# Value products of two attention quads given back to back at every second quad, with four probability slots

## The chip, the cores and the metric

The kernel runs on one core of a Trainium2 chip. The metric is the device time of one execution in microseconds (us). The kernel before has a median of 1106.15 us over 3 runs (1104.24 to 1106.32).

## The reference

Two transformer layers, each with the norm behind the residual sum, on x of shape (2, 1024, 256), 16 heads of width 16, float32. Cut to what matters:

```python
# layer 0: causal attention, then a feed-forward with ternary weights
dots = einsum('bhid,bhjd->bhij', q, k) * scale ; causal mask
out  = einsum('bhij,bhjd->bhid', softmax(dots), v)
x = layernorm(x + out @ w_out + b_out) ; x = layernorm(x + ffn0(x))
# layer 1: 16 query heads, 4 key heads, slope times distance added to the scores,
# a band of +-32 around the diagonal and the first 64 rows and columns left out
qk = q k^T * scale + slope * (-|i - j|) ; qk = where(band or global, -1e9, qk)
out = softmax(qk) @ v
x = layernorm(x + out @ Wo + bo) ; x = layernorm(x + ffn1(x))
```

## The kernel before, in words

Each layer is a block in which five engines run in parallel, ordered by semaphores. The attention of a layer is cut into N = 8 groups: 2 batches times 4 groups of 4 heads (HG = 4). A group is cut into quads: one quad is one tile of 128 keys against one half (512) of the queries, for the 4 heads of the group. Layer 0 has 12 quads (half 0 has 4, half 1 has 8, since the mask is causal; near the diagonal a quad has 384, 256 or 128 columns instead of 512). Layer 1 has 16 quads, 8 of 448 columns and 8 of 512; the last of each half has 64 key rows. A step of a quad is:

- "exp": TensorE writes one head's shifted scores (`shifted`, lines 1039 to 1059) into a PSUM bank, and ScalarE writes their exponential into the probabilities `prob` (lines 1005 to 1007). There are two banks for this, 4 and 5 (`T_BANKS`, line 688), and four in the last group. TensorE waits before a shifted product until the exponential that used its bank is done (lines 1120 to 1122).
- "max": TensorE writes the scores of one head and 128 queries (`score`, line 1029) for the group that comes next, and VectorE takes the row maximum (lines 940 to 942), with two slots of two banks each. There are 32 such units per group, 2 or 3 per quad.
- "values": TensorE multiplies the quad's probabilities with the values (`values`, lines 1061 to 1079). Each head is a product with 32 output rows, so four heads stand side by side in the array and write bank 6 in four strips. They are float32 and read as 8 records. Line 1135 waits for GpSimd's mask (lines 871 and 877) where the quad touches the diagonal or the band.
- "evict": ScalarE copies bank 6 to SBUF at the end of each half (line 1014). "norm": TensorE transposes the copy (line 1147) and VectorE divides (lines 971 and 973).

The function `plan` (line 125 on) writes out by hand one order of these steps for a group, and every engine goes through that same list and does its own part. The values of quad n - 1 stand behind the exponentials of quad n. The values of a group's last quad, its last eviction and its last norm are done at the first and second quad of the group that follows.

`prob` holds two quads, quad q in slot q % 2. ScalarE waits before a quad's first exponential for the values of the quad two before (line 1003). SyncE loads the operands of a later group when the values of the one before are all done (line 814), and GpSimd stages values then (line 883). The last group also has the preparation of the output projection in its list (`with_preparation`).

Of the kernel before, what the change touches and what calls it, by code (L numbers as in the profile page):

```python
# [20 lines left out]
F32 = mybir.dt.float32  # L21
# [4 lines left out]
P = 128  # L26
# [6 lines left out]
HG = 4  # L33
NG = H // HG
N = B * NG
E = 1024
KE = E // P
CH = 512
# [86 lines left out]
def plan(layer, group):  # L125

    quads = quads_of(layer)
    nq, nu = len(quads), len(units_of(layer))
    rows_at = nq - KEY_TILES_AHEAD[layer.index]
    lead = nu * KEY_TILES_AHEAD[layer.index] // nq  # L130
    stream = [(k, 1) for k in range(lead if group >= 1 else 0, nu)] if group + 1 < N else []
    stream_next = [(k, 2) for k in range(lead)] if group + 2 < N else []
    late, last = group >= 1, group == N - 1
    steps, given, given_next = [], 0, 0
    tail = [("values", nq - 1), ("evict", 1), ("norm", 1)]
    for n, (half, kt) in enumerate(quads):
        due = min(len(stream), -(-len(stream) * (n + 1) // rows_at))
        due_next = -(-len(stream_next) * (n + 1 - rows_at) // (nq - rows_at)) if n >= rows_at else 0
        if n == rows_at and stream:
            steps.append(("parts", 0, 1))  # L140
        for h in range(HG):
            steps.append(("exp", HG * n + h, 0))
            upto = given + -(-(due - given) // (HG - h))
            steps += [("max", u, later) for u, later in stream[given:upto]]
            given = upto
            upto = given_next + -(-(due_next - given_next) // (HG - h))
            steps += [("max", u, later) for u, later in stream_next[given_next:upto]]
            given_next = upto
        if n == 0 and late:
            steps += [(what, k, -1) for what, k in tail[:2]]  # L150
        if n == 1 and late:
            steps.append((*tail[2], -1))
        if n == 1 and not last:
            steps.append(("stage", 0, 1))
        if group <= 2 and layer.index == 1 and n in CUT_QUADS:

            steps.append(("cut", 2 * group + CUT_QUADS.index(n), 0))
        if n >= 1:
            steps.append(("values", n - 1, 0))
            if quads[n - 1][0] != half:  # L160
                steps.append(("evict", quads[n - 1][0], 0))
        if n >= 2 and quads[n - 2][0] != quads[n - 1][0]:
            steps.append(("norm", quads[n - 2][0], 0))
        if n == rows_at and stream:
            steps.append(("rows", 0, 1))
        first = RESIDUAL_GROUP[layer.index]
        if first <= group < first + 4 and n in RESIDUAL_QUADS[layer.index]:
            steps.append(("residual", 4 * (group - first) + RESIDUAL_QUADS[layer.index].index(n), 0))
    if last:
        steps += [(what, k, 0) for what, k in tail]  # L170
        steps = with_preparation(steps, nq)
    return steps
# [498 lines left out]
def attend(nc, sem, K, L, dram, prep, before):  # L671


    i = L.index
    tag = str(i)
# [4 lines left out]
    NU, NX, NQ = len(units), HG * len(quads), len(quads)  # L680
# [11 lines left out]
    MH = HG if i == 0 else HG // 2  # L692
# [17 lines left out]
    values_done = sem("values_done" + tag)  # L710
# [4 lines left out]
    with ExitStack() as st:  # L715
        table, maxes, vst, prob, mpart, mrow, ot, rec = (K.table, K.maxes, K.vst, K.prob, K.mpart, K.mrow, K.ot, K.rec)
# [5 lines left out]
            before.proj = proj  # L722
        opening = opening_of(L, proj)

        def exp_slots(n):
            return LAST_T_BANKS if n == N - 1 else T_BANKS

# [93 lines left out]
        def _(pool):  # L821
# [38 lines left out]
            def step(group, steps):  # L860
                for what, k, later in steps:
                    n = group + later
                    if what == "exp" and k % MH == MH - 1 and diagonal[k // HG] is not None:

                        pool.wait_ge(exp_done, n * NX + (k + 1))
                        half, kt = quads[k // HG]
                        a, b = diagonal[k // HG]
                        j0, rows = key_tile(L, kt)
                        cells = prob[0:rows, k // HG % 2, k % HG + 1 - MH:k % HG + 1, a - half * CH:b - half * CH]
                        if i == 0:  # L870
                            nc.gpsimd.affine_select(out=cells, in_=cells, pattern=[[0, HG], [1, P]],  # L871
                                                    compare_op=ALU.is_ge, fill=zero, base=0, channel_multiplier=-1
                                                    ).then_inc(masked, 1)
                        else:
                            off = a - (j0 - WIN)
                            bits = cells.bitcast(I32)
                            nc.gpsimd.tensor_tensor(bits, bits, keep[0:rows, off:off + b - a].unsqueeze(1)  # L877
                                                    .to_broadcast((rows, MH, b - a)), ALU.mult
                                                    ).then_inc(masked, 1)
                    elif what == "stage":  # L880
                        if group >= 1:

                            pool.wait_ge(values_done, group * NQ)
                        if n == NG:

                            pool.wait_ge(proj.v_done, (2 - i) * len(proj.v_units))
                        stage(n, n % BUFS)
                    elif what == "cut":

                        j, cols = k // 2, slice(k % 2 * E, (k % 2 + 1) * E)  # L890
                        pool.wait_ge(w_loaded, 16 * (j + 1))
                        nc.gpsimd.tensor_copy(K.wffn[:, j, 0, cols], wf[:, cols]).then_inc(w_cut, 1)
                        pool.wait_ge(w_cut, 2 * k + 1)
                        nc.gpsimd.tensor_tensor(K.wffn[:, j, 1, cols], wf[:, cols],
                                                K.wffn[:, j, 0, cols].bitcast(F32), ALU.subtract).then_inc(w_cut, 1)
                    elif what == "residual":
                        if k == 0:

                            pool.wait_ge(proj.xt_full, len(proj.turns))
                            pool.wait_ge(K.tri_loaded, 16 * 5)  # L900
                        nc.gpsimd.tensor_tensor(K.x[:, k, :], K.x[:, k, :], K.bias[:, i, :], ALU.add
                                                ).then_inc(residual, 1)
                    elif what == "inverse":
                        prep.inverse(pool, k, 0)
                    elif what in Projection.STEPS:
                        proj.pool(pool, what, k)
                    elif what in FeedForward.STEPS:
                        before.pool_tail(pool, what, k)
# [83 lines left out]
        def _(act):  # L992
            def step(group, steps):
                for what, k, later in steps:
                    n = group + later
                    if what == "exp":
# [1 line left out]
                        lo, hi = columns_of(L, half, kt)  # L998
                        rows = key_tile(L, kt)[1]
                        q = k // HG  # L1000
                        if k % HG == 0 and n * NQ + q >= 2:

                            act.wait_ge(values_done, n * NQ + (q - 1))
                        act.wait_ge(t_full, n * NX + (k + 1))
                        nc.scalar.activation(prob[0:rows, q % 2, k % HG, lo % CH:lo % CH + hi - lo],  # L1005
                                             ps[0:rows, t_bank(n, k), lo % CH:lo % CH + hi - lo],
                                             ACT.Exp).then_inc(exp_done, 1)
                    elif what == "evict":
# [19 lines left out]
        def _(pe):  # L1028
# [29 lines left out]
                        start = False  # L1058
                return last

            def values(qd, par):

                half, kt = quads[qd]
                lo, hi = columns_of(L, half, kt)
# [9 lines left out]
                for h in range(HG):  # L1074
                    last = nc.tensor.matmul(ps[32 * h:32 * h + 32, O_BANK, lo % CH:lo % CH + hi - lo],  # L1075
                                            vst[:, par, vt_, h % v_heads, :],
                                            prob[:, qd % 2, h, lo % CH:lo % CH + hi - lo],
                                            start=opening and not uniform, stop=True, skip_group_check=True)
                return last

            def step(group, steps):
                for what, k, later in steps:
# [41 lines left out]
                    elif what == "values":  # L1124
# [8 lines left out]
                        pe.wait_ge(exp_done, n * NX + HG * (k + 1))  # L1133
                        if diagonal[k] is not None:
                            pe.wait_ge(masked, HG // MH * (n * upto[-1] + upto[k]))
                        values(k, b).then_inc(values_done, 1)
                    elif what == "norm":
                        pe.wait_ge(evicted, n * 2 + (k + 1))

# [445 lines left out]
def memory(shared, at, L):  # L1585
# [20 lines left out]
    K.kop = at((101632, 122112)[i], "kop" + tag, [P, BUFS, L.key_sets, T], BF16)  # L1606
    K.vst = at((126208, 164992)[i], "vst" + tag, [P, BUFS, TB + i, v_heads, 2 * HD], F32)
    K.prob = at(171392, "prob" + tag, [P, 2, HG, CH], F32)
    K.maxes = at((23040, 164864)[i], "maxes" + tag, [P, HG, TB], F32)
    K.mpart = at((22528, 168448)[i], "mpart" + tag, [P, 2, P // 2], BF16)  # L1610
    K.mrow = at((22784, 168704)[i], "mrow" + tag, [P, P], BF16)
# [110 lines left out]
```

## Time and profile before

| | before |
|---|---|
| median of 3 runs | 1106.15 us (1104.24 to 1106.32) |
| the profiled execution's own time | 1099.92 us |
| its span | 1098.2 us |
| mean granted TensorE clock | 0.973 |
| TensorE busy | 994.7 us (91%) |
| VectorE busy | 697.1 us (63%) |
| ScalarE busy | 605.9 us (55%) |
| GpSimd busy | 346.5 us (32%) |
| attention groups, layer 0 | from 84 to 355 us of the span |
| attention groups, layer 1 | from 535 to 941 us of the span |

PE is TensorE, PEld its weight loads, ACT is ScalarE, DVE VectorE, POOL GpSimd. Matmuls are pipelined and the ends of their records are modelled, so a busy TensorE is not TensorE at its peak, and the start of a record tells more than its end. A row of the timeline merges neighbouring instructions of one kind on one engine: its start is that of the first, its duration reaches to the end of the last, and x gives their number. The brackets at a row's end hold the idle time of the engine before it and what ended it.

### The profile page before, as it was taken

The page shows a single profiled execution, that of the slowest core. Times are in us where ns is not written, and L with a number is a line of the kernel's source. Part 1 is how long each engine was busy: PE and PEld are TensorE (multiplying, and loading weights), DVE is VectorE, ACT ScalarE, POOL GpSimd, SP SyncE. Part 2 cuts the span into 40 slices and gives each one's busy share as a digit, 9 for nine tenths or more (in the row PEclk, how much of TensorE's full clock was granted, in tenths as well). Part 3 has the DMA queues.
Part 4 walks back from the last instruction along what each step waited for, and adds up shares of the span by engine and source line. Part 5 has one row for each costly group of instructions (what it writes and reads, how often), then busy time and mean ns, then how long its engine had stood idle before and what let it go on. Part 6 is the DMA issues. An engine that isn't in the chain of part 4 may idle for free. (4 is left out here: it accounts for less than half of the span.)

```text
span 1098.2 us, 17969 instructions
## 1 busy us (share of the span) xinstructions
PE 994.7 (91%) x6546; PEld 517.9 (47%) x6546; DVE 697.1 (63%) x1535; ACT 605.9 (55%) x1204; POOL 346.5 (32%) x414
## 2 busy tenths in 40 slices
PE   6688999999988999877799999999999999899995
PEld 4342333333324788653333343433334344698885
DVE  2877877777735566457787777777777724235322
ACT  4335666676665434333566777777776767323321
POOL 3031312222211434321344353524334252324331
PEclk9898999999999899997899999999999999999999
DMA  7552110112000200024433050303211000000001
GB/s 252 168 172 70 59 43 18 59 58 59 2 1 1 74 15 1 23 90 110 148 94 133 30 162 2 124 4 121 71 54 36 1 2 1 1 1 20 20 1 39
DMA packets 32979, 64.19 MB, mean 58 GB/s; under 512 B 6079, under 2 KB 22351, under 8 KB 30516
## 3 DMA queue, kind: packets, MB, share of 16 engines
q1 hardware_dynamic: 31548, 58.47, 17.3%
q0 software_dynamic: 1072, 3.80, 1.0%
q8 instruction: 52, 0.85, 0.3%
q10 hardware_dynamic: 272, 0.79, 0.2%
q14 instruction: 35, 0.29, 0.1%
HBM read 50.45 MB, written 12.32 MB: 57 GB/s over the span
## 5 line engine op out<-in xcount | busy, mean ns | idle before, releaser
L1005 ACT ACTIVATE prob<-ps 128x512 f32<-128x512 f32 (+6 forms) x896 | 442.7, 537 | 211.4 <-PE ps L1048 203.7
L1048 PE MATMUL ps<-qop,kop 98*128 98x512 bf16 (+15 forms) x1376 | 302.4, 291 | 21.3 <-ACT prob L1005 7.6
L1034 PE MATMUL ps<-kop,qop 96*128 96x512 bf16 (+3 forms) x896 | 255.7, 359 | 33.2 <-DVE maxes L940 26.6
L1048 PEld LDWEIGHTS ps<-qop,kop 107*128 107x128 bf16 (+2 forms) x1376 | 114.4, 98 | 278.2 <-ACT prob L1005 200.7
L1075 PE MATMUL ps<-prob,vst 128*32 128x512 f32 (+4 forms) x1792 | 211.2, 543 | 3.9 <-POOL prob L877 2.6
L940 DVE CUSTOM_DVE_ANT_0 sums<-ps,tri 128x128 bf16<-128x128 f32 (+7 forms) x256 | 183.7, 754 | 43.6 <-PE ps L1034 42.3
L940 DVE CUSTOM_DVE_ANT_0 sums<-ps,table 128x960 bf16<-128x960 f32 x128 | 148.0, 1156 | 80.4 <-PE ps L1034 65.8
L877 POOL TENSOR_TENSOR prob<-prob,keep 128x384 int32<-128x384 int32 (+2 forms) x144 | 122.6, 853 | 220.7 <-ACT prob L1005 218.2
L1466 PE MATMUL ps<-xs,wffn 128*128 128x512 f32 x640 | 157.0, 401 | 3.7 <-PEq L715 2.2
L940 DVE CUSTOM_DVE_ANT_0 tri<-ps,table 128x960 bf16<-128x960 f32 x128 | 147.5, 1152 | 3.6 <-PE ps L1034 3.5
L1466 PEld LDWEIGHTS ps<-xs,wffn 128*128 128x128 f32 x640 | 120.4, 191 | 31.5 <-issue 5.1
L1367 POOL TENSOR_TENSOR hs<-hf,hs 128x512 fp32r<-128x512 f32 x64 | 82.8, 1295 | 158.8 <-ACT hs L1393 158.2
L1034 PEld LDWEIGHTS ps<-kop,qop 96*128 96x128 bf16 x896 | 79.0, 99 | 104.1 <-DVE maxes L940 58.6
L871 POOL TENSOR_SCALAR_AFFINE_SELECT prob<-prob 128x512 f32<-128x512 f32 x64 | 40.9, 639 | 205.8 <-ACT prob L1005 205.8
L1487 PE MATMUL ps<-wffn,hs 128*128 128x256 f32 x640 | 80.6, 287 | 7.1 <-POOL hs L1367 7.1
L1487 PEld LDWEIGHTS ps<-wffn,hs 128*128 128x128 f32 x640 | 78.9, 195 | 9.1 <-POOL hs L1367 8.4
L1393 ACT CAST hs<-hf 128x512 fp32r<-128x512 f32 x64 | 39.3, 614 | 72.4 <-PE ps L1487 66.3
L1075 PEld LDWEIGHTS ps<-prob,vst 128*32 128x32 f32 x1792 | 35.7, 108 | 50.9 <-issue 35.1
L1431 DVE SCALAR_TENSOR_TENSOR hf<-ps,sg 128x512 f32<-128x512 f32 x32 | 22.0, 690 | 46.6 <-PE ps L1466 46.6
L1400 ACT ACTIVATE sg<-ps 128x512 f32<-128x512 f32 x32 | 19.2, 599 | 54.0 <-PE ps L1466 54.0
L940 DVE DVE_READ_ACCUMULATOR2_ANT maxes<- 128x1 f32 x512 | 42.4, 83 | 0.0
L615 PE MATMUL ps<-prob,w 128*128 128x512 f32 x80 | 38.0, 607 | 1.3 <-DVE staging L542 1.3
(103 smaller groups left out, 686.4 us busy)
## 6 DMA issues: line engine op xcount, KB each, us to landing
table<-in_table SPq DMA_DIRECT2D x32, 464.0 KB, 5.1
qop<-q_parts SPq DMA_DIRECT2D x96, 128.0 KB, 2.6
kop<-k_parts SPq DMA_DIRECT2D x48, 128.0 KB, 2.6
kop<-k_parts SPq DMA_DIRECT2D x48, 96.0 KB
q_parts<-qop SPq DMA_DIRECT2D x8, 384.0 KB, 2.9
q_parts<-kop SPq DMA_DIRECT2D x8, 384.0 KB, 2.6
x<-in_x SPq DMA_DIRECT2D x4, 512.0 KB, 5.5
out<-x SPq DMA_DIRECT2D x4, 512.0 KB, 2.9
```

Source lines behind the costliest of these rows:

```text
L615: last = nc.tensor.matmul(ps[:, self.bank(what, k), :], w[:, half, m * P:(m + 1) * P], src[:, half, t0:t0 + CH], start=(half == 0), stop=( ...
L871: nc.gpsimd.affine_select(out=cells, in_=cells, pattern=[[0, HG], [1, P]], compare_op=ALU.is_ge, fill=zero, base=0, channel_multiplier=-1) ...
L877: nc.gpsimd.tensor_tensor(bits, bits, keep[0:rows, off:off + b - a].unsqueeze(1) .to_broadcast((rows, MH, b - a)), ALU.mult).then_inc(mask ...
L940: nc.vector.tensor_tensor_reduce(out=sums[k % 2][:, lo:hi], in0=scores, in1=mask, scale=1.0, scalar=LOWEST, op0=ALU.add, op1=ALU.max, accu ...
L1005: nc.scalar.activation(prob[0:rows, q % 2, k % HG, lo % CH:lo % CH + hi - lo], ps[0:rows, t_bank(n, k), lo % CH:lo % CH + hi - lo], ACT.Ex ...
L1034: last = nc.tensor.matmul(ps[:, S_BANK + 2 * (k % S_SLOTS) + a // CH, a % CH:a % CH + b - a], qop[0:RD, par, h, i0:i0 + P], kop[0:RD, par, ...
L1048: return nc.tensor.matmul(ps[0:rows, bank, a % CH:a % CH + b - a], lhs, rhs, start=start, stop=True, skip_group_check=True)
L1075: last = nc.tensor.matmul(ps[32 * h:32 * h + 32, O_BANK, lo % CH:lo % CH + hi - lo], vst[:, par, vt_, h % v_heads, :], prob[:, qd % 2, h, ...
L1367: nc.gpsimd.tensor_tensor(self.hidden(e, 1), hf[:, u % 2, :], self.hidden(e, 0).bitcast(F32), ALU.subtract).then_inc(self.h_lo, 1)
L1393: nc.scalar.copy(self.hidden(e, 0), hf[:, u % 2, :]).then_inc(self.h_hi, 1)
L1466: last = nc.tensor.matmul(ps[:, 2 * (u % 2) + which, :], weights[a][:, k, e * P:(e + 1) * P], prep.xs[:, c % 2, b, k, :], start=(n == 0), ...
L1487: last = nc.tensor.matmul(self.K.ps[:, 4 + half, (j % 2) * D:(j % 2 + 1) * D], self.hidden(e, b)[:, j * P:(j + 1) * P], self.wdown[a][:, e ...
```

## The change

The values of two quads are given together. In groups 0 to 6, at quads n = 2, 4, 6, ..., the values of quads n - 2 and n - 1 are given one behind the other, and at odd quads none are given. The values of the last two quads of a group are given at the first quad of the next group, with the eviction behind them. The last group keeps its single quads, one behind the exponentials.

The probabilities get a second array of the same size, `prob_far`, so that quad q of groups 0 to 6 has slot q % 4; the last group uses the two slots of `prob` as before. ScalarE's wait before a quad's exponentials is for the values of the quad four before (two before in the last group, from its third quad on). The order of exponentials, maxima, evictions and norms within the list is the same.

```diff
@@ plan
     tail = [("values", nq - 1), ("evict", 1), ("norm", 1)]
+    pair = [("values", nq - 2), *tail]
...
         if n == 0 and late:
-            steps += [(what, k, -1) for what, k in tail[:2]]
+            steps += [(what, k, -1) for what, k in pair[:3]]
         if n == 1 and late:
-            steps.append((*tail[2], -1))
+            steps.append((*pair[3], -1))
...
+        if last and n >= 1:
+            steps.append(("values", n - 1, 0))
+        elif not last and n >= 2 and n % 2 == 0:
+            steps += [("values", n - 2, 0), ("values", n - 1, 0)]
         if n >= 1:
-            steps.append(("values", n - 1, 0))
             if quads[n - 1][0] != half:
                 steps.append(("evict", quads[n - 1][0], 0))
@@ attend
+        def tile(n, q):
+
+            slot = q % 2 if n == N - 1 else q % 4
+            return (prob if slot < 2 else K.prob_far)[:, slot % 2, :, :]
@@ gpsimd, the mask
-                        cells = prob[0:rows, k // HG % 2, k % HG + 1 - MH:k % HG + 1, a - half * CH:b - half * CH]
+                        cells = tile(n, k // HG)[0:rows, k % HG + 1 - MH:k % HG + 1, a - half * CH:b - half * CH]
@@ scalar, the exponential
-                        if k % HG == 0 and n * NQ + q >= 2:
-
-                            act.wait_ge(values_done, n * NQ + (q - 1))
+                        back = 2 if n == N - 1 and q >= 2 else 4
+                        if k % HG == 0 and n * NQ + q >= back:
+
+                            act.wait_ge(values_done, n * NQ + (q + 1 - back))
...
-                        nc.scalar.activation(prob[0:rows, q % 2, k % HG, lo % CH:lo % CH + hi - lo],
+                        nc.scalar.activation(tile(n, q)[0:rows, k % HG, lo % CH:lo % CH + hi - lo],
@@ tensor, values
-                                            prob[:, qd % 2, h, lo % CH:lo % CH + hi - lo],
+                                            tile(n, qd)[:, h, lo % CH:lo % CH + hi - lo],
@@ memory
     K.prob = at(171392, "prob" + tag, [P, 2, HG, CH], F32)
+    K.prob_far = at((49152, 77056)[i], "prob_far" + tag, [P, 2, HG, CH], F32)
```

## Rows read from the trace of the kernel before

**Rows 1.** Page, busy us (share of the span) xinstructions of each engine.

```profile
PE 994.7 (91%) x6546; PEld 517.9 (47%) x6546; DVE 697.1 (63%) x1535; ACT 605.9 (55%) x1204; POOL 346.5 (32%) x414
```

**Rows 2.** Busy time in two stretches: one group of layer 0, one of layer 1.

```profile
259.43:292.44 33.01, 30.49 (x203) 10.42 (x201) 24.81 (x72) 22.35 (x50) 5.63 (x9) 1.00 0.14 41
700.31:749.38 49.07, 48.35 (x391) 18.28 (x390) 38.19 (x72) 35.28 (x67) 18.41 (x25) 1.00 0.22 70
```

**Rows 3.** Waits: who waited for whom, us in total, times, longest.

```profile
ACT prob L1005 <- PE ps L1048: 203.7, 260, 8.0
PEld ps L1048 <- ACT prob L1005: 200.7, 443, 1.0
```

**Rows 4.** Timeline of one quad, layer 1, first half: start us, us, engine line op.

```profile
709.58 0.96 PE L1075 MATMUL ps<-prob,vst 128*32 128x448 f32 x8
...
710.47 0.10 PEld L1048 LDWEIGHTS ps<-qop,kop 107*128 107x128 bf16 x1 [0.73 <-ACT prob L1005]
...
710.67 0.57 PE L1034 MATMUL ps<-kop,qop 96*128 96x448 bf16 x2
...
710.93 2.12 ACT L1005 ACTIVATE prob<-ps 128x448 f32<-128x448 f32 x4 [0.67 <-PE ps L1048]
711.08 0.35 PE L1048 MATMUL ps<-qop,kop 107*128 107x448 bf16 x1
...
711.38 1.16 DVE L940 CUSTOM_DVE_ANT_0 sums<-ps,table 128x960 bf16<-128x960 f32 x1 [0.63 <-issue]
...
712.07 0.10 PEld L1048 LDWEIGHTS ps<-qop,kop 107*128 107x128 bf16 x1 [0.44 <-ACT prob L1005]
...
712.36 0.96 PE L1075 MATMUL ps<-prob,vst 128*32 128x448 f32 x8
...
712.46 1.15 DVE L940 CUSTOM_DVE_ANT_0 tri<-ps,table 128x960 bf16<-128x960 f32 x1
```

**Rows 5.** Timeline of one quad, layer 1, second half.

```profile
727.57 1.06 PE L1075 MATMUL ps<-prob,vst 128*32 128x512 f32 x8
...
728.56 0.40 PE L1048 MATMUL ps<-qop,kop 107*128 107x32 bf16 x2
...
729.06 2.30 ACT L1005 ACTIVATE prob<-ps 128x512 f32<-128x512 f32 x4 [0.76 <-PE ps L1048]
729.21 0.39 PE L1048 MATMUL ps<-qop,kop 107*128 107x32 bf16 x2
...
730.29 0.11 PEld L1048 LDWEIGHTS ps<-qop,kop 107*128 107x128 bf16 x2 [0.34 <-ACT prob L1005]
...
730.62 1.07 PE L1075 MATMUL ps<-prob,vst 128*32 128x512 f32 x8
```

**Rows 6.** Timeline of an eviction and of the turn of its output.

```profile
721.08 0.96 PE L1075 MATMUL ps<-prob,vst 128*32 128x448 f32 x8
...
722.11 0.59 ACT L1014 COPY ot<-ps 128x512 f32<-128x512 f32 x1 [0.29 <-PE ps L1075]
...
722.59 2.17 ACT L1005 ACTIVATE prob<-ps 128x512 f32<-128x512 f32 x4
...
724.06 1.07 PE L1075 MATMUL ps<-prob,vst 128*32 128x512 f32 x8
...
725.55 0.38 PE L1048 MATMUL ps<-qop,kop 107*128 107x512 bf16 x1
```

**Rows 7.** Timeline of layer 0: value products of 128 columns.

```profile
289.75 0.42 PE L1075 MATMUL ps<-prob,vst 128*32 128x128 f32 x8
...
290.10 0.34 PE L1048 MATMUL ps<-qop,kop 98*128 98x384 bf16 x1
```

**Rows 8.** Timeline of the quad with 64 key rows, layer 1.

```profile
716.03 0.38 PE L1048 MATMUL ps<-qop,kop 107*64 107x448 bf16 x1
...
716.85 0.38 PE L1048 MATMUL ps<-qop,kop 107*64 107x448 bf16 x1
```

More of the change, by code:

```diff
@@ L1059, in shifted, with values @@
                 return last
-            def values(qd, par):
+            def values(n, qd, par):
                 half, kt = quads[qd]
@@ L1135, in step @@
                             pe.wait_ge(masked, HG // MH * (n * upto[-1] + upto[k]))
-                        values(k, b).then_inc(values_done, 1)
+                        values(n, k, b).then_inc(values_done, 1)
                     elif what == "norm":
```

## The prediction

> **What bounds the kernel now.** I read the busy shares first, then the two attention stages by window, then the waits, then the timeline of single quads. The page shows TensorE busy 91% of the span and ScalarE 55% [rows 1], which invites the reading "TensorE is the bound". One group of 12 quads in layer 0 takes 33.01 us and one of 16 quads in layer 1 takes 49.07 us, at full granted clock, with TensorE busy 30.49 and 48.35 us [rows 2]. But a busy record includes the time in which a matmul drains, and the waits tell another story: ScalarE waited 203.7 us for the shifted scores of line 1048, and TensorE's weight loads for that line waited 200.7 us for ScalarE's exponentials [rows 3]. Two engines that wait for each other by the same amount are in a loop.
>
> The timeline shows the loop [rows 4]. Call s0 to s3 the four shifted products of a quad, e0 to e3 their exponentials, V a quad's value products, m a maximum's score product. V starts at 709.58. s0 follows at 710.47, 0.89 later. e0 starts at 710.93, 0.46 after s0, and ScalarE had been idle for 0.67. Four exponentials take 2.12, 0.53 each. There are two score banks, so s3 can't be given before e1 is done: that is at 710.93 + 1.06 = 711.99, and the weights of s3 load at 712.07, 0.08 later, after an idle 0.44 put down to ScalarE. The next V follows at 712.36, 0.29 later. So the period is 0.89 + 0.46 + 1.06 + 0.08 + 0.29 = 2.78 us, and each term is a step that waits for the one before. e2 and e3 are not in it: they run beside V. In the second half of layer 1, with 512 columns, the same sum is 0.99 + 0.50 + 2 x 0.575 + 0.08 + 0.33 = 3.05 us [rows 5]. TensorE has slack in it: beside V it is the two-bank hand-over with ScalarE that sets the pace.
>
> **The change, part by part.** It removes, adds and moves no arithmetic. At each second quad it gives two sets of value products one behind the other, and none at the quad between. The groups concerned are 0 to 6 of each layer: 7 x 6 = 42 pairs in layer 0 and 7 x 8 = 56 in layer 1, 98 in all.
>
> Gained by pairing: one exit from the value products and one entry. After V of 128 columns the next product starts 0.35 later [rows 7]; after 512 columns, 0.99 [rows 5]. That is 0.64 for 384 columns, 0.00167 us each, which is four passes at 2.4 GHz. So 128 columns stream for 0.21 and the exit costs 0.14. At the entry V starts 0.29 behind s3, where the score product m starts 0.20 behind s0 [rows 4]: 0.09. Together 0.23 per pair. The cost of V behind V appears in no row. It is at least the streaming, 0.75 for 448 columns, and at most the streaming with exit and entry, 0.98. I take 0.75, since between two V nothing changes in the shape of the tiles, and keep the other end for the range.
>
> Lost by pairing: the cover of e2 and e3. Chain of a pair in the first half of layer 1, from the first V at 0. The second V at 0.75, s0 at 0.75 + 0.89 = 1.64, e0 at 2.10 to 2.63. Meanwhile ScalarE still has only two exponentials to do, since the banks are two as before: e2 and e3 of the last quad end at 0.70, so it idles for 1.40, and twice the old 0.67 is 1.34. The longer pause gives nothing back. s1 follows s0 by 0.61, as 711.08 after 710.47 [rows 4], since m lies between; s1 2.25, e1 2.71 to 3.24; s2 at 2.86, e2 3.32 to 3.85; s3 waits for e1: 3.32, e3 3.85 to 4.38. No V here: the next quad's s0 needs the bank of e2, 3.85 + 0.08 = 3.93, e0 4.39 to 4.92; s1 4.54 (0.61 behind), e1 5.00 to 5.53; s3 at 5.61, V at 5.90. Two old periods are 5.57. So **+0.33 us per pair**: two more exponentials on the path (1.06) and 0.24 of TensorE pacing, against one 0.46 + 0.08 + 0.29 and the exit of 0.14 saved.
>
> For the second half, with 0.64 from s0 to s1 (729.21 after 728.56 [rows 5]): streaming 0.85 + 0.99 = 1.84, e0 2.34, e1 2.98 to 3.56, e2 3.62 to 4.20, next s0 4.28, e0 4.78, s1 4.92, e1 5.42 to 5.99, s3 6.07, V 6.40, against 6.10: **+0.30**.
>
> The quads with 64 key rows stand at the end of each half of layer 1, before the boundary. Their s0 to s1 is 0.82 instead of 0.61 [rows 8]. Singly that delays the loop once (0.21), in a pair twice: +0.21 more, two per group.
>
> The eviction and the turn (norm) come twice per group. Before, ScalarE's copy starts 0.07 after V ends and holds the next exponential for 0.48 [rows 6]; it lies in the pause. In a pair the second V ends at 0.85 + 1.06 = 1.91, so the copy starts at 1.98 and e0 at 2.46 instead of 2.34: 0.12 lost, and e0 is what is queued behind it. The four transposes stretched V to s0 to 1.49 (724.06 to 725.55 [rows 6]), 0.50 more than 0.99. In the new order they follow a quad that has no V: s3 at 3.76, plus 0.20, plus 0.50 gives 4.46 instead of s0 at 4.28. Total 0.18 lost where about 0.46 was paid before (3.51 from V at 724.06 to V at 727.57 against 3.05 [rows 5, 6]): a gain of 0.27, two per group, 0.54.
>
> The other queues. VectorE: maxima follow each other by 1.08 (711.38 to 712.46 [rows 4]), 4.3 in a pair of 5.9, and the first starts 0.71 behind its m (710.67 to 711.38): m at 1.84 and 2.45 end at about 3.7 and 4.8, the third m (4.13) finds its slot free, the fourth (4.74) waits for 4.87, which moves s2 and not s3. Free; if VectorE were 0.4 later it would set V. GpSimd's masks of the second quad must be there at 5.90, and e3 of that quad ended at 4.38, against 0.70 and 2.78 before: a little less margin, still 1.5 us. SyncE's operand loads and GpSimd's staging wait for the last values of a group, now one V (0.9 us) later, a group (33 or 49 us) ahead of need. Four slots for the probabilities: ScalarE's wait is for values two pairs back, never last. All three at nothing; the cover is the group's length.
>
> Sum. Layer 1, per group: 4 x 0.33 + 4 x 0.30 + 0.42 - 0.54 = 2.40, times 7 = 16.8. Layer 0, per group, with full quads like those of the second half (its short quads have shorter exponentials but then wait for the wide maxima): 6 x 0.30 - 0.54 = 1.26, times 7 = 8.8. Total **+25.6 us**. The last groups, the projections and the feed-forward are the same code. On the profiled execution, 1099.92 us with a span of 1098.2, that gives 1125.5. That execution is 6.2 below the median of 1106.15 and under the lowest of the three runs (1104.24). From the median: 1131.8, said as 1132.
>
> The Trainium skill, TensorEngine Tiling (Array Packing), Key Properties, says that changing the tiling mode, not just the tile, drains the TensorEngine. The exit of 0.14 [rows 5, 7] agrees. By that rule alone the change is a gain; what it would give is the first rival.
>
> **Rivals.** (1) *TensorE is the bound after all, and the drain saved is time saved.* 98 x 0.23 = 22.5 us less: 1083.6. For it: 48.35 busy of 49.07 [rows 2]. Against it: the idle 0.67 before e0 and 0.44 before s3 in each quad [rows 4], and the period that adds up without any TensorE work but V and s3. It decides if ScalarE's exponentials ran ahead of TensorE, that is, if s0 to s3 of the quad without V didn't wait for their banks. Chance 0.10.
> (2) *A draw.* The pacing of TensorE in the pair, 0.24, is hidden. Then a pair costs 6 x 0.53 + 1.64 + 0.46 + 0.08 + 0.29 = 5.65, +0.08, and in the second half +0.10; 98 x 0.09 - 28 x 0.27 = 1.3 us: 1107.5. For it: the queue of TensorE may give s1 early, since its bank is free. Against: rows of each quad show 0.61 with m between. Chance 0.07.
> (3) *The second V pays exit and entry like the first*, 0.23 more: +22.5, so 1154. For it: each V set ends with a signal and begins with waits. Against: they are met by then. Chance 0.06.
> (4) That the pairs aren't formed can't be: each engine's order is written out.
> The forecast has the rest, 0.77.
>
> **How the numbers follow.** Within the forecast, layer 0 may be 0 to 2.5 a group and the V behind V may cost some 0.15 more, which is 1115 to 1148. The range goes down to the draw at its lower part, 1108, and leaves out (1), most of what lies within 0.2% (2.2 us, about what a measurement of this kernel can tell from no change) and the top of (3). Faster: (1), and the low side of (2), 0.11. Same: the rest of (2), 0.06. Slower: 0.83.
>
> **What the new profile would show.** V sets starting 0.75 or 0.85 apart in pairs, then 5.9 us to the next pair in layer 1's first half and 6.4 in its second; a layer 1 group of 51.5 us and a layer 0 group of 34.3. ScalarE idle about 1.4 before the first exponential behind a pair, and almost none at the next quad. Exit rows between V and V gone. The turn's transposes off the path. I am wrong if the pair's period is under 5.57: then e0 to e3 of the quad between were not the path. I am wrong in a term if V to V isn't 0.75, or if s0 of the second quad starts later than 2.29 after that of the first (3.93 less 1.64).

## Result and profile after

The changed kernel takes 1125.22 us (median of 4 runs, 1121.18 to 1126.49), against 1105.2 for the kernel before beside it (1101.87 to 1106.32): a ratio of 1.0183, 95% interval [1.0151, 1.0215], so 20 us more. The profiled execution took 1124.03 us with a span of 1122.3; its counterpart of before had 1099.92 and 1098.2, so the two traces lie 24.1 us apart. The forecast was 25.6 more. The sign and the mechanism held; the sizes of several terms did not, and a term that the forecast didn't have, the granted clock, made up for part of what it had put too high.

The work is the same, as the page after shows (engine busy us, share, instructions), to be held against [rows 1]:

```profile
PE 995.3 (89%) x6546; PEld 531.8 (47%) x6546; DVE 694.3 (62%) x1535; ACT 609.7 (54%) x1204; POOL 346.3 (31%) x414
```

TensorE and ScalarE are busy for nearly as long as before (0.6 and 3.8 us more), in a span 24.1 us longer: nearly all of the time is waiting. By stretches (us, then PE, PEld, DVE, ACT, POOL busy, granted clock, DMA share, GB/s), group 0 of layer 0, one steady group of layer 0 and one of layer 1; the last two answer to [rows 2]:

```profile
85.37:134.16 48.79, 41.73 (x229) 13.95 (x230) 34.26 (x98) 26.96 (x57) 6.27 (x10) 0.87 0.15 43
236.26:270.30 34.04, 30.20 (x203) 11.16 (x202) 24.90 (x72) 22.75 (x50) 8.39 (x13) 1.00 0.15 45
719.77:769.74 49.97, 47.51 (x393) 19.15 (x390) 37.93 (x72) 35.29 (x67) 18.38 (x25) 1.00 0.22 69
```

The same stretch of group 0 in the kernel before, from its first shifted product to the same norm:

```profile
84.58:127.38 42.80, 39.01 (x230) 13.09 (x230) 34.42 (x98) 26.31 (x57) 6.28 (x10) 0.93 0.16 49
```

A steady group costs 1.03 us more in layer 0 and 0.90 more in layer 1, at full clock in both. Group 0 of layer 0 costs 6.0 more, at a lower granted clock (0.87 against 0.93). Followed through the trace, the first feed-forward starts 14.4 us later than before (0.8 of it before the attention, 6.0 in group 0, 5.1 in the next five groups, 2.5 in the rest), the output of layer 1's attention 22.6 later, and the end 24.1. The 0.8 ahead of the attention and the last 1.5 lie in code that the change leaves alone.

One pair in the timeline after, answering to [rows 4] (start us, us, engine line op):

```profile
726.42 1.71 PE L1085 MATMUL ps<-prob_far,vst 128*32 128x448 f32 x16
...
728.06 0.36 PE L1058 MATMUL ps<-qop,kop 107*128 107x448 bf16 x1
...
728.52 2.11 ACT L1015 ACTIVATE prob<-ps 128x448 f32<-128x448 f32 x4 [1.30 <-PE ps L1058]
...
729.27 0.75 PE L1058 MATMUL ps<-qop,kop 107*128 107x448 bf16 x2
...
730.25 0.36 PE L1058 MATMUL ps<-qop,kop 107*128 107x448 bf16 x1 [0.23 <-ACT prob L1015]
...
730.71 1.08 ACT L1015 ACTIVATE prob_far<-ps 128x448 f32<-128x448 f32 x2
...
731.26 0.11 PEld L1044 LDWEIGHTS ps<-kop,qop 96*128 96x128 bf16 x2 [0.48 <-DVE maxes L949]
...
731.68 0.54 PE L1058 MATMUL ps<-qop,kop 107*128 107x448 bf16 x2
...
731.85 0.10 PEld L1058 LDWEIGHTS ps<-qop,kop 107*128 107x128 bf16 x1 [0.28 <-ACT prob_far L1015]
...
732.15 1.71 PE L1085 MATMUL ps<-prob,vst 128*32 128x448 f32 x16
```

The two value sets stand together (16 records, 1.71 us), and s0 comes 1.64 behind their start, as forecast. ScalarE was idle for 1.30 before e0 (forecast 1.40). The second quad's s0 waits for ScalarE (the idle 0.23) and comes at 3.83 behind V (forecast 3.93). The next V is at 5.73 (forecast 5.90), against 5.57 for two single periods. Two waits end at the same moment before it. The fourth maximum's product waits for VectorE until 731.26, which puts s2 at 731.68 and s3 right behind it, at 731.87, and e1 ends in time for the weights of s3 at 731.85. So in this pair VectorE sets the last part of the path as much as ScalarE does.

### The profile page after: what moved, and what is told of

It is laid out like the page before. It is cut to its first block and busy times, and to the rows that moved or that the text cites. A ratio compares the mean times of both kernels' runs of the same rounds, so it can differ in the third digit from the quotient of the medians.

```text
span 1122.3 us, 17965 instructions
## 1 busy us (share of the span) xinstructions
PE 995.3 (89%) x6546; PEld 531.8 (47%) x6546; DVE 694.3 (62%) x1535; ACT 609.7 (54%) x1204; POOL 346.3 (31%) x414
## 5 line engine op out<-in xcount | busy, mean ns | idle before, releaser
L1015 ACT ACTIVATE prob<-ps 128x512 f32<-128x512 f32 (+2 forms) x504 | 258.3, 562 | 94.7 <-PE ps L1058 88.9
L1015 ACT ACTIVATE prob_far<-ps 128x512 f32<-128x512 f32 (+5 forms) x392 | 186.4, 503 | 119.9 <-PE ps L1058 113.1
L1085 PE MATMUL ps<-prob,vst 128*32 128x512 f32 (+2 forms) x1008 | 118.5, 579 | 3.9 <-POOL prob L886 2.6
L886 POOL TENSOR_TENSOR prob_far<-prob_far,keep 128x384 int32<-128x384 int32 (+2 forms) x70 | 52.8, 755 | 174.3 <-ACT prob_far L1015 173.7
L886 POOL TENSOR_TENSOR prob<-prob,keep 128x384 int32<-128x384 int32 (+3 forms) x74 | 69.7, 944 | 55.8 <-ACT prob L1015 54.0
L1085 PE MATMUL ps<-prob_far,vst 128*32 128x512 f32 (+3 forms) x784 | 78.7, 520 | 0.0
L880 POOL TENSOR_SCALAR_AFFINE_SELECT prob<-prob 128x512 f32<-128x512 f32 x36 | 23.2, 644 | 166.6 <-ACT prob L1015 166.6
L1085 PEld LDWEIGHTS ps<-prob,vst 128*32 128x32 f32 x1008 | 25.8, 110 | 51.6 <-issue 40.1
```

What stands on the lines that cost most here:

```text
L1015: nc.scalar.activation(tile(n, q)[0:rows, k % HG, lo % CH:lo % CH + hi - lo], ps[0:rows, t_bank(n, k), lo % CH:lo % CH + hi - lo], ACT.Exp ...
```

## Experiments

All medians of before below come from runs beside the kernel in question.

**One layer at a time.** A function `paired(layer, group)` decides which groups give values in pairs; the others give them singly, with four slots.

```diff
+def paired(layer, group):
+    return 0 <= group < N - 1 and layer.index == 1      # second kernel: == 0
...
-        if last and n >= 1:
+        if not paired(layer, group) and n >= 1:
             steps.append(("values", n - 1, 0))
-        elif not last and n >= 2 and n % 2 == 0:
+        elif paired(layer, group) and n >= 2 and n % 2 == 0:
```

> Pairs in layer 1 alone, single quads in layer 0. The loop theory (a pair lengthens the chain shifted product, exponential, shifted product, because the last two exponentials of the quad between lose their cover): a group of layer 1 takes 49.96 us as with the full change, against 49.07 before, so 7 x 0.9 and the end of the last group, 6 to 8 us over before, and layer 0's groups take 33.01. Rival, the second probability array or four slots cost by themselves: layer 0's groups are longer too (they also use four slots here), and the total is nearer 14.

Measured: ratio 1.0069 [1.0049, 1.0089], 1112.03 us against 1105.24, 6.8 more. The windows, a group of layer 0 and one of layer 1:

```profile
259.53:292.62 33.09, 30.57 (x203) 10.42 (x202) 24.81 (x72) 22.46 (x50) 5.63 (x9) 1.00 0.15 45
708.62:758.58 49.96, 47.49 (x391) 19.12 (x389) 37.93 (x72) 35.27 (x67) 18.35 (x25) 1.00 0.21 67
```

Layer 1 has the change's group, layer 0 that of before.

> Pairs in layer 0 alone, single quads in layer 1. The loop theory: layer 0's groups take 34.03 instead of 33.01, 7 us in all, and layer 1's take 49.07. The clock theory (pairs make TensorE pause longer at the start of layer 0 and the granted clock falls to half there, where the first group took 6 us more): another 6 us on top, 12 to 14 in all over before, with a granted clock of half speed in a stretch of group 0 or 7. Without the clock's part: 7.

Measured: ratio 1.0115 [1.0095, 1.0136], 1117.12 us, 11.9 more, just under the span expected with the clock's part and well over the 7 without it.

```profile
268.32:302.37 34.05, 30.27 (x204) 11.16 (x201) 24.81 (x72) 22.99 (x50) 5.63 (x9) 1.00 0.13 40
714.04:763.10 49.06, 48.34 (x390) 18.27 (x389) 38.19 (x72) 35.28 (x67) 18.40 (x25) 1.00 0.22 70
```

The mirror image. 6.8 and 11.9 add up to 18.7 of the 20, which is the whole within the intervals, and layer 0 has the larger part. These two runs also separate the order from the clock. Counted from the first exponential of a group to that of the next, layer 1's groups together took 6.9 us more in the first run, with no fall of the granted clock in them beyond that at their start, which the kernel before has too. In the second run groups 1 to 6 of layer 0 took 1.02 to 1.04 more each, and group 0 took 3.9 more (41.95 against 38.01), with one fall of the clock at 94.5 us. The full change has that fall and another at 118.4, and its group 0 took 5.6 more (43.59): one such fall costs 1.6 us here.

**Slots alone.** `paired` returns False; the two arrays and the wait four quads back stay.

> Four slots and the looser wait of ScalarE, values of single quads as before. The loop theory: no change, within 2 us of before, since ScalarE never waited last for the values. Rival, the far array costs something by its place: 7 x 12 + 7 x 16 quads, half of them in the far array, would cost above 2 us.

Measured: ratio 0.9993 [0.9976, 1.0009], 1103.8 us against 1105.24. The far array and the looser wait cost and give nothing. All of the loss comes from the order of the value products and from what that order brings about.

**A longer third product, a longer first product.** The most direct test of "TensorE isn't the bound, the loop is" puts the same added work at two places of the kernel before.

```diff
+                        if k % HG == 2 and n < N - 1:      # second kernel: == 0
+                            shifted(k, b, t_bank(n, k))
                         shifted(k, b, t_bank(n, k)).then_inc(t_full, 1)
```

> The kernel before; in groups 0 to 6 of both layers TensorE gives the third shifted product of each quad twice, to the same bank (the output is the same). That adds 0.19 to 0.22 us of TensorE work to 196 quads, some 36 us. The loop theory: it lies in the time in which TensorE waits for e1, so it costs 0 to 0.05 a quad, 0 to 8 us. Rival, TensorE's work is the bound: 30 to 40 us.

> The same for the first shifted product of each quad, which lies on the loop between the values and the first exponential. The loop theory and its rival both expect the full 0.17 to 0.22 a quad, 30 to 42 us; only together with the run of the third product does it tell them apart.

Measured: the third product twice, ratio 1.0067 [1.0043, 1.0091], 8.0 us more (1111.41 against 1103.4). The first product twice, ratio 1.032 [1.0291, 1.0349], 36.3 more. In the windows, first with the third product doubled, a group of layer 0 and one of layer 1:

```profile
263.45:297.06 33.61, 31.69 (x214) 11.10 (x213) 24.81 (x72) 22.31 (x50) 5.63 (x9) 1.00 0.14 41
708.99:758.49 49.50, 49.50 (x421) 20.24 (x421) 38.41 (x72) 35.31 (x67) 18.40 (x25) 1.00 0.21 69
```

and with the first doubled:

```profile
268.50:303.00 34.50, 32.09 (x215) 11.50 (x214) 24.85 (x72) 22.35 (x50) 5.63 (x9) 1.00 0.14 40
724.58:776.86 52.28, 51.62 (x422) 20.43 (x421) 38.38 (x72) 35.61 (x67) 18.43 (x25) 1.00 0.21 66
```

In layer 1 the same work costs (49.50 - 49.06) / 16 = 0.03 us a quad at one place and (52.28 - 49.06) / 16 = 0.20 at the other. With the third product doubled, layer 1's window has TensorE busy for 49.50 of 49.50 us and still took almost all of the added work for nothing: busy time that the records fill isn't the bound. The rival of the prediction, that TensorE's own work decides, falls here.

The same on the changed kernel:

> The full change with the third shifted product of each quad given twice in groups 0 to 6 (same output). Single quads paid 8.0 us for it, 0.04 a quad. The loop theory: in a pair the third product of the first quad is on the path, since the next quad's first product waits for the bank of e2, and that of the second quad delays the fourth product (the one before the values) by what is beyond the end of e1: 0.2 and 0.1 to 0.2 a pair, 98 pairs, 25 to 40 us over the change (45 to 60 over before). Rival, TensorE keeps the slack in pairs that it has in single quads: 8 us over the change (28 over before).

Measured: ratio 1.0328 [1.0292, 1.0365] to before. The change alone is at 1.0183, so 16 us over it, where single quads paid 8. It lies between the two expectations. The trace says which half was right:

```profile
737.77 1.71 PE L1085 MATMUL ps<-prob_far,vst 128*32 128x448 f32 x16
...
739.42 0.36 PE L1058 MATMUL ps<-qop,kop 107*128 107x448 bf16 x1
...
741.80 0.36 PE L1058 MATMUL ps<-qop,kop 107*128 107x448 bf16 x1 [0.42 <-ACT prob L1015]
...
742.62 0.11 PEld L1044 LDWEIGHTS ps<-kop,qop 96*128 96x128 bf16 x2 [0.29 <-DVE maxes L949]
```

The second quad's s0 stands at 4.03 behind V instead of 3.83. That is the first quad's third product, on the path as expected, 0.20 a pair. The group of layer 1 took 51.52 us, 1.56 over the change's for 8 pairs: 0.20 each, and nothing for the second quad. There the fourth maximum's product comes 0.82 behind s0, at 742.62, still waiting for VectorE, where it came 1.01 behind in the change (731.26 after 730.25): the second quad starts 0.20 later and VectorE doesn't, so the added product finds the 0.19 that the wait for VectorE had taken up, and s3 again stands 1.62 behind s0. So the theory was right on the first quad of a pair and wrong on the second.

**Maxima behind the second product.** The prediction put 0.24 us of the pair on TensorE's pacing, because a maximum's score product stands between s0 and s1. In single quads this can be taken away.

```diff
-            upto = given + -(-(due - given) // (HG - h))
+            upto = (given, min(due, given + 2), due, due)[h]      # the same for stream_next
```

> The kernel before with one thing moved: the first maximum of a quad stands behind the second shifted product instead of between the first and the second, so s1 follows s0 by 0.20 us instead of 0.61. The loop theory: e1 then starts as soon as ScalarE is free and ends about 0.10 earlier, and s3 and the next values with it: 0.08 to 0.10 per quad of layer 1 (112 quads), 9 to 11 us, and between nothing and 8 us in layer 0, where the wide maxima come late: 9 to 19 us less in all. Rival, TensorE's own work is the bound: the order inside a quad changes nothing, within 2 us of before. Third case: the two maxima side by side make VectorE the late one, and it is slower.

Measured: ratio 1.0015 [0.9995, 1.0035], 1105.14 against 1105.24: no change, so the expected 9 to 19 us was missed. (Two of the twelve executions took 1112.7 and 1113.1 at a mean granted clock of 0.953, the other ten 1103.8 to 1106.8.) The trace shows two effects that cancel. A group of layer 1 takes 47.48 instead of 49.07, 0.10 a quad, as expected. A group of layer 0 takes 33.74 instead of 33.01 (the next expectation says 33.47, a misreading of these 33.74), which I put down to the wide maxima, up to three a quad, without a run that shows it. Group 0 of layer 0 takes 3.6 more (41.57 against 38.01 from first exponential to first exponential), with the granted clock at its lower level until 96.5 us instead of 90.4, and group 0 of layer 1 gained nothing. So the move was tried in layer 1 alone, and on top of the change. In the next kernels all maxima of a quad stand behind the second product, `(given, due, due, due)[h]`, where above a third one stood behind the third.

> The kernel before with single quads; in layer 1 alone both maxima of a quad stand behind the second shifted product. With late maxima in both layers a group of layer 1 took 47.47 us instead of 49.06 and one of layer 0 33.47 instead of 33.01. The loop theory: layer 1's gain alone is kept, 7 x 1.6 = 11 us less than before (median near 1094). Rival, the median of 1105.1 with both was no sum of a gain and a loss: no change, within 2 us.

> The full change with the same move of the maxima in layer 1. The loop theory with VectorE in it: the pair's path is then s0 (V+1.64), e2's end (V+3.78), the next s0 (V+3.83), and the fourth maximum's product can't start before VectorE has done the second (V+4.98), so s2 and s3 of the second quad come at 5.5 and 5.7 and the next V at 5.9 to 6.0 instead of 5.73: a group of layer 1 takes 50 to 52 us, no gain over the change (0 to 10 us more), where single quads gain 1.6 a group. Rival, TensorE's pacing is all that costs in the pair: it gains as single quads do, 5.63 a pair and 8 to 11 us less than the change.

Measured, single quads: ratio 0.9968 [0.995, 0.9985], 1099.75 against 1103.4, 3.6 less and not 11. The steady groups took 47.48, but group 0, which has 32 maxima over 13 quads, took 54.7 instead of 53.3 between two marks (the first product with `ones` of group 0 and that of group 1). From the first exponential of the one to that of the other it is more: 57.8 instead of 54.5. The granted clock stood at its lower level for the first 8.8 us of it, until 552.3, and in the kernel before for the first 4.9, until 547.8. So the loss in group 0 is one of the clock too.

Measured, pairs: ratio 1.0273 [1.0245, 1.0301], about 10 us over the change, at the top of what was expected. Here the move gains nothing, and the timeline has the reason:

```profile
735.53 1.71 PE L1086 MATMUL ps<-prob_far,vst 128*32 128x448 f32 x16
...
737.17 0.55 PE L1059 MATMUL ps<-qop,kop 107*128 107x448 bf16 x2
...
739.36 0.80 PE L1059 MATMUL ps<-qop,kop 107*128 107x448 bf16 x2 [0.34 <-ACT prob L1016]
...
740.56 0.11 PEld L1045 LDWEIGHTS ps<-kop,qop 96*128 96x128 bf16 x2 [0.46 <-DVE maxes L950]
...
741.45 1.71 PE L1086 MATMUL ps<-prob,vst 128*32 128x448 f32 x16
```

The next s0 stands at V+3.83 and the next V at V+5.92, both as written down before. The fourth maximum waits for VectorE (the idle 0.46) and carries the last two shifted products with it. VectorE is busy for 62% of the change's span, yet four maxima squeezed into the part of a pair without values find two slots full. The steady group is 50.04 us, no more than 0.1 over the change's. Nearly all of the 10 us is in group 0 of layer 1 (58.6 instead of 53.6 between the marks, 63.9 instead of 55.1 from first exponential to first exponential). There the granted clock stayed at its lower level until 572.9, the first 15.7 us of the group, where the change has it for 4.9, and fell once more at 593.3.

> Late maxima in layer 1 from group 1 on, single quads. With late maxima in all of layer 1 the steady groups gained 1.58 each, but group 0, which has 32 maxima over 13 quads, took 54.68 instead of 53.30, and the median gained 3.6 only. The loop theory with VectorE in it: group 0 returns to 53.3, the others keep 1.58, so 1 to 2 us under the run with late maxima everywhere and 5 to 9 under before. Rival, group 0's 1.4 was chance: same as that run, 3 to 4 under before.

Measured: ratio 0.9926 [0.99, 0.9952], 1096.03 us against 1106.03. By the ratio that is 8 us less than before, within the 5 to 9 expected, and 4 to 5 under the run with late maxima everywhere, where 1 to 2 was expected: the marks had shown only part of what group 0 lost. Group 0 of layer 1 is back at 53.2 us between the marks, and at 54.5 from first exponential to first exponential, with 5.3 us at the lower clock at its start. The steady groups keep their gain:

```profile
701.76:749.25 47.49, 47.32 (x391) 18.34 (x390) 38.05 (x72) 33.95 (x67) 18.42 (x25) 1.00 0.22 72
```

This version, single quads with the maxima behind the second product in layer 1 from group 1 on, beats both kernels.

**The clock in group 0.**

> The full change, but group 0 of each layer keeps single quads. The full change is 20 us over before. Of its groups 1 to 6, layer 0 gives 6 x 1.03 and layer 1 6 x 0.9, 11.6 us. The clock theory: in layer 0's group 0 the profiled execution showed a granted clock of 0.84 against 0.93 from 84 to 127 us and took 6 us more instead of 1; without pairs there that goes, so 11 to 14 us over before, and group 0 has before's clock. Rival, the falls of the clock are chance and not the pairs': still 18 to 20 over before.

Measured: ratio 1.0125 [1.0098, 1.0152], 12.8 us over before and 6 to 7 under the change, within the 11 to 14 expected. The granted clock is the third number from the end of a window's row. The change comes first, in four stretches of group 0 of layer 0,

```profile
90.00:96.00 6.00, 4.61 (x24) 1.46 (x25) 5.18 (x16) 2.54 (x7) 1.82 (x3) 0.78 0.55 154
96.00:102.00 6.00, 4.85 (x27) 1.21 (x19) 3.44 (x7) 1.86 (x6) 0.63 (x1) 0.84 0.00 1
...
114.00:120.00 6.00, 4.70 (x23) 1.21 (x27) 4.57 (x14) 3.57 (x6) 0.63 (x1) 0.87 0.00 0
120.00:126.00 6.00, 5.30 (x30) 1.62 (x22) 3.22 (x8) 2.89 (x7) 0.63 (x1) 0.85 0.02 3
```

and with single quads in group 0:

```profile
90.00:96.00 6.00, 5.92 (x36) 1.96 (x35) 5.09 (x17) 2.58 (x8) 1.83 (x3) 0.86 0.52 171
96.00:102.00 6.00, 4.86 (x36) 1.79 (x35) 5.67 (x16) 3.48 (x8) 0.63 (x1) 1.00 0.00 1
...
114.00:120.00 6.00, 5.66 (x34) 1.85 (x34) 3.61 (x13) 4.28 (x11) 1.27 (x2) 1.00 0.02 3
120.00:126.00 6.00, 5.14 (x43) 1.96 (x44) 5.02 (x16) 3.70 (x11) 1.27 (x2) 1.00 0.00 0
```

With pairs the clock fell to its lower level (1.2 GHz of 2.4) for part of these stretches, twice in group 0, each time behind waits of TensorE for VectorE of 0.3 to 0.8 us. Two pairs of value sets fell into it and took 3.18 and 3.61 us, where one of full width takes 1.92 at full clock. Without pairs the clock stayed full from 96 us to the end of the group. That pairs bring these falls on, in this place, is shown by taking them away, and the other traces agree: the four kernels with pairs in group 0 of layer 0 have one or two falls there (one with pairs in layer 0 alone and in the change with late maxima, two in the change and in the change with the third product doubled), and of the nine without pairs there none has one, apart from the kernel with late maxima in layer 0, whose low clock at the start of the group lasts longer.

The 6 to 7 us aren't all the clock's. Two falls at 1.6 each are 3.3 in the change's group 0 of layer 0. The rest of its 5.6 is order: the 1.03 of a steady group, and more waiting for VectorE (from 84 us on to the end of the group TensorE's matmuls waited 5.7 us for it, against 2.3 before). Group 0 of layer 1 took another 0.65 to 0.9. Falls came elsewhere as well: the change's profiled execution has one at 330 us, at the end of group 6 of layer 0 (1.9 us in that group and the next, against the run with pairs in layer 0 alone), and one at 906.9, in group 6 of layer 1 (1.7 against the run with pairs in layer 1 alone). Neither is in the run that it is compared with, while the kernel with single quads in group 0 has one at 323.8, so what brings these two on isn't shown.

## Why the prediction was right, and where its terms were off

**The loop.** Right. The path runs from the values over s0, e0 and e1 to s3, and pairing puts e2 of the first quad and e0 and e1 of the second behind one another, without cover. The doubled products show it in the kernel before and, for the first quad, in the changed one.

**V behind V and the exit.** Right: the change's s0 comes 1.64 behind V, so the second set costs its streaming, 0.75, and rival 3 falls. An exit of 0.14 is saved per pair, and is worth less than what it uncovers.

**The pair's 0.33 and 0.30.** Right in sign, twice too large: 5.73 against 5.57, +0.16, in the first half of layer 1, and 6.26 and 6.24 against 6.09 and 6.13, +0.17 and +0.11, in the second. The step that failed is the 0.24 of TensorE pacing. I took the 0.46 between s0 and e0 for every product. It holds behind the values. In a running quad s2 at 729.27 gave e2 at 729.66, 0.39. The path from s0 to the next s0 was 2.19 instead of 2.29 (0.07 of it the earlier e2, 0.03 the hand-over from e2 to s0, 0.05 instead of 0.08), and from there to V 1.90 instead of 1.97. So the pacing cost 0.10 and not 0.24. With +0.16 the pair came out nearer to the second rival's +0.08, which had the pacing at nothing, than to the forecast's +0.33. The same mistake hid in the 0.53 taken for the length of an exponential. In the kernel before, e1 started 0.39 behind its s1 at 711.08: it was paced by TensorE. With the maxima moved, e0 and e1 stood 0.44 apart (716.14 and 716.58), with records of 0.54. That ScalarE's instructions overlap when they stand back to back agrees with the Trainium skill, ScalarE: Activation LUTs, What ACT_TABLE_LOAD costs, which gives about 93 ns; here it is 0.10 us.

**The quads of 64 rows.** Right: their windows grew by 0.38 (5.93 to 6.31) and 0.45 (6.19 to 6.64), about 0.2 to 0.3 over a plain pair, where 0.21 was forecast.

**Eviction and turn.** Right in kind, undersized. The window with the first turn fell from 6.49 to 6.08 and the one with the second from 7.09 to 6.97. Against the plain pair of their half (+0.16 and +0.14 on the mean) that is 0.57 and 0.26, 0.4 each on the mean and not 0.27.

**The sums.** Layer 1: 0.90 a group and 8.2 us in the trace, against 2.40 and 16.8. Layer 0: 1.03 a group, near the 1.26, but 13.6 us (14.4 less the 0.8 ahead of the attention) against 8.8. The prediction had no term for the clock. By the prices above, the clock took about 3.3 in group 0 of layer 0, 1.9 at that layer's end and 1.7 in layer 1, an estimate of 6.9 from one execution, and the order of the value products the other 15. Layer 1 was 8.6 too high and layer 0 4.8 too low. With the 2.3 outside the attention the total was 1.5 above the traces' 24.1, and it was 5.6 above the medians' 20. The forecast of the total was better than its parts, and that was luck. The order alone cost some 15 us where 25.6 was forecast: 8.4 in layer 0, near the 8.8, and 6.5 in layer 1 instead of 16.8. The clock, which had not been forecast, filled part of the gap.

**Work costed at nothing.** The slots, the far array and the looser waits cost nothing (the run with slots alone). VectorE was put at nothing with a margin of 0.4, and that was wrong. The prediction's own numbers leave less: a fourth maximum's product at 4.87 puts s2 at 5.28 (0.41 behind it, as in both traces) and s3 at 5.47, against 5.61. In the trace that product came at 4.84, and with s3 at 5.45 no margin was left. In the pairs with late maxima VectorE set V.

**The range.** 1125.2 lies in it, and in the forecast's own 1115 to 1148.

## What to carry to other kernels

Where two engines hand work to each other through two buffers, write down the loop that both wait in before counting the busy time of either; batching a third kind of work on one of them saves its switching cost once and takes away the cover that it gave to the other. Test it by doubling a small instruction at two places of the loop: what costs nothing at one and everything at the other isn't work but order. A latency read behind a pause isn't the latency in a running stream, and a start spacing read off a timeline may be the pace of the producer and not the length of the consumer's work.

## What the runs showed that was not expected

The granted clock fell to half in part of group 0 of layer 0 with pairs and stayed full there with single quads; giving single quads back to the first group of each layer returned 6 to 7 of the 20 us, about half of it by the clock. TensorE's records covered 49.50 of 49.50 us in a group that had taken in 16 more shifted products for 0.43 us. And the best place found for a gain, 0.10 us a quad by moving a maximum behind the second product, was no gain at all in layer 0, in group 0 of layer 1 and in the pairs: in the pairs the trace shows a slot of VectorE's coming last, and in the two group 0s the low clock at their start lasted longer.
